# Attention in trips of 64 queries of four batches, with float32 scores in tiles

## The reference

```python
qkv = x @ c_attn_w + c_attn_b                      # q, k, v of the words
k = concat([cond @ uk_w.T + uk_b, k]); v = concat([cond @ uv_w.T + uv_b, v])
scores = q @ k.T / sqrt(32)                        # 16 heads, causal: kj <= qi + 1
x1 = x + (softmax(scores + mask) @ v) @ c_proj_w + c_proj_b
xw = x1 @ Wx + b
h = tanh(h @ Wh + xw[t])                           # 512 steps, all batches at once
out = x1 + h
```

## Time and profile before

| | us |
|---|---|
| three runs, median | 1697.04 (1691.76 to 1697.95) |
| the profiled execution | 1689.44 |
| its span, first to last instruction | 1687.6 |
| PE busy | 1521.2 (90%) |
| PE weight loads | 1288.2 (76%) |
| DVE, ACT, POOL busy | 817.9, 718.4, 369.9 (48%, 43%, 22%) |

### The profile page before, as it was taken

The page is one execution under the profiler, slowest core; times in us unless marked ns, Lnnn a source line. Parts: engine busy times, 40 slices in busy tenths (PEclk is TensorE's granted clock), DMA queues, the critical chain, the costliest instruction groups (busy, mean ns, idle before and its releaser), DMA issues.

```text
span 1687.6 us, 65682 instructions
## 1 busy us (share of the span) xinstructions
PE 1521.2 (90%) x28397; PEld 1288.2 (76%) x28397; DVE 817.9 (48%) x2592; ACT 718.4 (43%) x2289; POOL 369.9 (22%) x535
## 2 busy tenths in 40 slices
PE   6589988999999999999999988999999999777775
PEld 6478777778877878888888877888888788666664
DVE  4455554454545455555555545555565555222221
ACT  3355553444444444544445444454454545111111
POOL 2045552203131222203132130311313100000000
PEclk9799899999999999999999999999999999999999
DMA  7655555334344454445545445555555632000000
GB/s 252 184 186 179 166 181 145 111 96 124 106 126 116 120 145 132 129 110 144 143 137 151 112 136 148 142 156 133 151 140 156 165 89 70 9 15 10 15 9 15
DMA packets 139936, 204.73 MB, mean 121 GB/s; under 512 B 19432, under 2 KB 91240, under 8 KB 139136
## 3 DMA queue, kind: packets, MB, share of 16 engines
q1 hardware_dynamic: 112640, 128.05, 28.9%
q0 software_dynamic: 27008, 72.47, 13.0%
HBM read 133.06 MB, written 67.37 MB: 119 GB/s over the span
## 4 chain that ended last, share of the span: by engine, by line
PE 79%; DMA 6%; DVE 5%; issue 4%; ACT 4%; SPq 2%; POOL 0%; DVEq 0%; ACTq 0%; POOLq 0%
PE rec L1004 24%; PE turned L938 10%; PE dense L466 7%; PE dense L467 6%; PE dense L468 6%; PE rec L995 5%; PE scores L928 5%; PE pv L951 4%; PE scores L1004 4%; DMA xin<-x 3%; DVE pre L842 3%; ACT states L694 2%; PE pv L969 2%; DMA kq<-kq_dram 1%; PE dense L1011 1%
## 5 line engine op out<-in xcount | busy, mean ns | idle before, releaser
L1004 PE MATMUL rec<-wh,states 128*32 128x128 f32 x14336 | 485.2, 276 | 62.9 <-ACT states L694 61.3
L1004 PEld LDWEIGHTS rec<-wh,states 128*32 128x32 f32 x14336 | 376.0, 110 | 129.1 <-ACT states L694 90.7
L648 ACT ACTIVATE probs<-probs,nmax 128x128 f32<-128x128 f32 (+3 forms) x512 | 287.4, 562 | 209.5 <-DVE nmax L791 203.0
L694 ACT ACTIVATE states<-pre 128x32 f32<-128x32 f32 x512 | 133.3, 260 | 431.3 <-DVE pre L842 430.3
L842 DVE STREAM_TRANSPOSE pre<-rec 128x128 f32<-128x128 f32 x448 | 141.6, 316 | 342.1 <-PE rec L1004 338.9
L791 DVE CUSTOM_DVE_ANT_0 probs<-scores,msk,nimg 128x128 f32<-128x128 f32 (+3 forms) x512 | 276.2, 544 | 61.8 <-PE scores L928 54.5
L938 PE MATMUL turned<-ident,probs 128*128 128x128 f32 x1280 | 243.7, 290 | 13.1 <-ACT probsT L655 11.7
L928 PE MATMUL scores<-kq 96*128 96x128 f32 (+3 forms) x512 | 204.9, 403 | 18.5 <-DMA kq<-kq_dram 16.7
L938 PEld LDWEIGHTS turned<-ident,probs 128*128 128x128 f32 x1280 | 145.4, 141 | 78.8 <-issue 55.7
L800 DVE COPY probsT<-turned 128x128 f32<-128x128 f32 (+3 forms) x256 | 124.6, 487 | 80.1 <-PE turned L938 75.7
L655 ACT COPY probsT<-turned 128x128 f32<-128x128 f32 (+3 forms) x256 | 107.0, 418 | 95.8 <-PE turned L938 94.2
(11 more groups left out here) (159 smaller groups left out, 2218.6 us busy)
## 6 DMA issues: line engine op xcount, KB each, us to landing
kq<-kq_dram SPq DMA_DIRECT2D x96, 320.0 KB, 5.2
kq<-kq_dram SPq DMA_DIRECT2D x96, 256.0 KB, 4.4
kq<-kq_dram SPq DMA_DIRECT2D x96, 192.0 KB, 3.6
kq_dram<-qs_hi POOLq DMA_DIRECT2D x120, 128.0 KB, 2.9
kq_dram<-ks_hi POOLq DMA_DIRECT2D x120, 128.0 KB, 3.4
kq<-kq_dram SPq DMA_DIRECT2D x96, 128.0 KB, 2.8
xin<-x SPq DMA_DIRECT2D x32, 256.0 KB, 4.0
v_dram<-vbuf POOLq DMA_DIRECT2D x32, 256.0 KB, 3.1
```

The lines of the kernel that those rows point to most:

```text
L648: act.activation(probs[:, g % PROBS, 0:n], probs[:, g % PROBS, 0:n], ACT.Exp, scale=-1.0, bias=nmax[:, e, h:h + 1], accum_out=rowsum[:, e, ...
L694: act.activation(state_cells(g), pre[:].rearrange("p f (b z) -> p f b z", z=GROUP)[:, :, :, s], ACT.Tanh).then_inc(h_ready, 1)
L1004: last = pe.matmul(rec_bank(g // GROUP)[Q * j:Q * j + Q, 0:P], state_tile(g - 1)[:, f, :], wh[:, f, P * j:P * j + P], start=False, stop=f ...
```

## The change

A trip is now 64 queries of four batches, `PARTS` = 8 parts by `QUADS` = 2, still 16 trips of 32 units. Part p sees 64 (p+1) keys, so the last stretch without attention has 64 steps, and 448 steps are spread over 14 trips. A unit is one head of two batches, 64 queries each, in the two halves of the 128 partitions.

- q stays in SBUF in float32; k is stored once in float32, by one DMA a chunk on SP's queue, and loaded by one DMA a group of four heads for two batches.
- A score is two float32 matmuls of 32 rows by 64 columns, one for each batch; head j of a group lies in rows 32 j. Units u and u+1 are put behind each other in PE's order.
- The values product has for each tile of keys and each head one matmul for each of two batches, of 64 columns each. Values are loaded in two or four DMAs into two buffers.
- A number of keys that is not a multiple of 128 leaves a last tile of 64 keys in transposes and values product.
- The image score is float32 on two tiles of 64 columns. x is loaded by four DMAs with runs of 64 queries. ACT makes q, DVE makes k. The split of x moves from unit 14 or 15 to 15 or 16, the chunks from 15 or 17 to 16 or 18.
- In the setup the raw weights lie elsewhere, and SP no longer waits ahead of the projection's weights.

```diff
-TRIPS = BLOCKS * PAIRS
+W = P // 2
+PARTS = S // W
+QUADS = 2
+PAIRED = 2
+TRIPS = PARTS * QUADS
 UNITS = 2 * H
 HEADS = TRIPS * UNITS
 GROUPS = HEADS // HC
-STEPS = S // (BLOCKS * PAIRS)
+STEPS = W // QUADS
...
-FIRST = (BLOCKS - 1) * P
-PROBS = 4
+FIRST = S - W
+PROBS = 5
 TURNED = 6
-ROOM = 2 * HC * (P + S)
+ROOM = 3 * 2 * S
 LOADS = 5
-FREE = (7, 5, 5, 5, 5)
-SPLIT_AT = (15, 14, 14, 14, 14)
-VTILES = 3
+SPLIT_AT = (16, 16, 15, 15, 15, 15, 15, 15)
+CHUNK_AT = (18, 18, 16, 16, 16, 16, 16, 16)
+VTILES = 2
...
-        size = HC * P * (block_of(group // 8) + 2)
+        size = 2 * keys(group // 8)
...
+            emit([("pv", v, 0, 0.1 + 0.213 * keys(v // 8) / P)])
         if TURN_LAG <= u < HEADS + TURN_LAG:
             v = u - TURN_LAG
-            emit([("turn", v, 0, 0.05 + 0.11 * (block_of(v // UNITS) + 1))])
+            emit([("turn", v, 0, 0.05 + 0.11 * tiles_of(v // UNITS))])
         if u < HEADS:
+            if u % 2 == 0:
+                emit([("score", v, 0, 0.07 + 0.107 * keys(g) / P) for v in (u, u + 1)])
             if u % HC == HC - 1:
                 loads += [("kqload", group, 0, 0.0) for group in range(GROUPS) if PLACES[group][0] == u // HC + 1]
-            emit([("score", u, 0, max(0.11, 0.053 * (block_of(g) + 1)) + 0.1)])
...
-        qs_hi = sb("qs_hi", [P, 2, 2 * P], F32R)
-        qs_lo = sb("qs_lo", [P, 2, 2 * P], F32R)
-        ks_hi = sb("ks_hi", [P, 2, 2 * P], F32R)
-        ks_lo = sb("ks_lo", [P, 2, 2 * P], F32R)
-        kq_tiles = sb("kq", [P, ROOM], F32R)
-        vbuf = sb("vbuf", [P, 2 * D + VTILES * BLOCKS * P])
+        q = sb("q", [P, 2, C, 2 * P])
+        knew = sb("knew", [P, C, 2 * P])
+        k_tiles = sb("kt", [P, ROOM])
...
-        kq_dram = nc.dram_tensor("kq_dram", [3, PAIRS, P, C, 2, P + S], F32, kind="Internal").ap()
+        k_dram = nc.dram_tensor("k_dram", [B, C, P, S], F32, kind="Internal").ap()
...
-        def store_parts(eng, kind, g, i):
-            p, r = divmod(g, PAIRS)
-            if kind == "q":
-                parts, at, stored = (qs_hi, qs_hi, qs_lo), 0, q_stored if g else q_stored_first
-            else:
-                parts, at, stored = (ks_hi, ks_lo, ks_hi), P * (p + 1), k_stored if g else k_stored_first
-            for part, src in enumerate(parts):
-                eng.dma_start(kq_dram[part, r, :, i, :, at:at + P],
-                              src[:, i % 2, :].bitcast(F32).rearrange("p (e t) -> p e t", e=2)
-                              ).then_inc(stored[i % 2], 16)
-        def wait_stored(eng, kind, parity, n):
-            first, later = (q_stored_first, q_stored) if kind == "q" else (k_stored_first, k_stored)
-            if n > 2:
-                eng.wait_ge(later[parity], 48 * (n - 2))
-            else:
-                eng.wait_ge(first[parity], 48 * n)
+        def store_keys(eng, g, i, stored):
+            p, r = divmod(g, QUADS)
+            eng.dma_start(k_dram[4 * r:4 * r + 4, i, :, W * p:W * p + W].rearrange("b p t -> p b t"),
+                          knew[:, i, :].rearrange("p (b t) -> p b t", b=4)).then_inc(stored, 16)
...
+        def load_x(eng, g):
+            p, r = divmod(g, QUADS)
+            for k in range(2):
+                for pair in range(PAIRED):
+                    eng.dma_start(xin[:, g % 2, pair, 2 * k:2 * k + 2, :].rearrange("p f (e t) -> p (f e) t", e=2),
+                                  x[p // 2 * PAIRS + 2 * r + pair, :, 2 * k:2 * k + 2, :]
+                                  .rearrange("p f (e t) -> p (f e) t", e=2)[:, :, W * (p % 2):W * (p % 2) + W]
+                                  ).then_inc(x_loaded[g % 2][k], 16)
...
-                    for part in range(3):
-                        sp.dma_start(heads_tile(g)[Q * part:Q * part + Q].bitcast(F32),
-                                     kq_dram[part, r, :, c, e, 0:P + P * (p + 1)]
-                                     .rearrange("(j d) t -> d j t", d=Q)).then_inc(tile_loaded[g % LOADS], 16)
+                    sp.dma_start(heads_tile(g), k_dram[4 * r + 2 * e:4 * r + 2 * e + 2, c, :, 0:keys(trip)]
+                                 .rearrange("b p t -> p b t")).then_inc(tile_loaded[g % LOADS], 16)
...
+                    whole, left = divmod(keys(trip), P)
+                    for b in range(2):
+                        mine = v_dram[4 * r + 2 * e + b, 0:keys(trip), P * c:P * c + P]
+                        if whole:
+                            sp.dma_start(vtile[g % VTILES][:, b, 0:whole, :],
+                                         mine[0:P * whole].rearrange("(n q) d -> q n d", q=P)
+                                         ).then_inc(v_loaded[g % VTILES], 16)
...
+                    act.activation(q[:, g % 2, i, :], bank(kind, g, i)[:, 0:2 * P], ACT.Identity,
+                                   bias=bqk[:, 0, i:i + 1]).then_inc(copied(kind, g, i), 1)
...
+                    dve.tensor_scalar(knew[:, i, :], bank(kind, g, i)[:, 0:2 * P], bqk[:, 1, i:i + 1], None,
+                                      ALU.add).then_inc(copied(kind, g, i), 1)
...
-                        pe.wait_ge(tile_loaded[group % LOADS], 48 * (group // LOADS + 1))
+                        if e == 0:
+                            wait_copied(pe, "q", trip, c)
+                        pe.wait_ge(tile_loaded[group % LOADS], 16 * (group // LOADS + 1))
                     if g > 1:
                         pe.wait_ge(shifted_ready, g - 1)
-                    pe.matmul(scores[g % 2][:, 0:n], heads_tile(group)[0:3 * Q, j, 0:P],
-                              heads_tile(group)[0:3 * Q, j, P:P + n], start=True, stop=True).then_inc(scores_ready, 1)
+                    rows = slice(Q * j, Q * j + Q)
+                    for b in range(2):
+                        at = W * (2 * e + b)
+                        last = pe.matmul(scores[g % 2][W * b:W * b + W, 0:n], q[rows, trip % 2, c, at:at + W],
+                                         heads_tile(group)[rows, b, :], start=True, stop=True, skip_group_check=True)
+                    last.then_inc(scores_ready, 1)
...
-                    for k in range(p + 1):
-                        last = pe.transpose(turned[g % 2][:, P * k:P * k + P], probs[:, g % PROBS, P * k:P * k + P], ident[:])
+                    for at in range(0, n, P):
+                        last = pe.transpose(turned[g % 2][0:min(P, n - at), at:at + P],
+                                            probs[:, g % PROBS, at:min(at + P, n)], ident[:])
...
-                    for k in range(p + 1):
-                        for j in range(HC):
-                            last = pe.matmul(pv[Q * j:Q * j + Q, P * c:P * c + P],
-                                             vtile[g % VTILES][:, k, Q * j:Q * j + Q],
-                                             probsT[:, (HC * g + j) % TURNED, P * k:P * k + P],
-                                             start=c == 0 and k == 0, stop=False, skip_group_check=True)
+                    for at in range(0, n, P):
+                        rows = slice(0, min(P, n - at))
+                        for b in range(2):
+                            mine = slice(at + W * b, at + W * b + W)
+                            for j in range(HC):
+                                last = pe.matmul(pv[Q * j:Q * j + Q, P * c + W * b:P * c + W * b + W],
+                                                 vtile[g % VTILES][rows, b, at // P, Q * j:Q * j + Q],
+                                                 probsT[rows, (HC * g + j) % TURNED, mine],
+                                                 start=c == 0 and b == 0 and at == 0, stop=False, skip_group_check=True)
```

More of the change, by code:

```diff
@@ L49 @@
 WEIGHT_LOADS = 16 * 2
[L50 removed]
+SETUP_LOADS = 16 * 9
 SPLITS = (0, 2, 4, 6, 1, 3, 5, 7)
 LAGS = {
[L56 removed]
+    "DVE": {"xsplit": 0.7, "k": 0.2, "v": 0.2, "imgscore": 0.2, "score": 0.2, "turn": 0.2, "imgprob": 0.0,
             "total": 0.5, "norm": 0.2, "attnlow": 0.9, "proj": 0.2, "step": 0.1, "hist": 0.8,
             "vimg": 0.2, "wproj": 0.8},
[L59 removed]
+    "ACT": {"xsplit": 0.0, "q": 0.2, "score": 0.8, "turn": 0.2, "imgprob": 0.2, "imgturn": 0.2,
             "rowturn": 0.2, "norm": 0.6, "step": 0.5, "out": 0.2, "wproj": 0.0},
[L61 to L62 removed]
+    "POOL": {"mskload": 0.9, "mskscale": 1.0, "vstore": 1.0, "out": 1.0, "vimg": 1.6},
+    "SP": {"xload": 0.8, "vimgload": 0.9, "k": 0.7, "kqload": 0.8, "vload": 0.5},
 }
@@ L68, in block_of, with keys, tiles_of @@
 def block_of(g):
-    return g // PAIRS
+    return g // QUADS
+def keys(g):
+    return W * (block_of(g) + 1)
+def tiles_of(g):
+    return -(-keys(g) // P)
 def tile_places():
@@ L86, with v_loads @@
 PLACES = tile_places()
+def v_loads():
+    counts = []
+    for group in range(GROUPS):
+        n = keys(group // 8)
+        mine = 2 * (n // P > 0) + 2 * (n % P > 0)
+        counts.append(mine + (counts[group - VTILES] if group >= VTILES else 0))
+    return counts
+V_LOADS = v_loads()
 def main_order():
@@ L176, in order @@
     place = {}
-    for b in range(BLOCKS - 1):
```

(41 more changed lines are left out.)

231 lines of the change are left out of this document (103 added, 128 removed).

## The result

The changed kernel takes 1740.35 us (median of four runs, 1732.76 to 1741.58), the kernel before 1695.55 (1691.76 to 1697.95): a ratio of 1.0257, 95% interval 1.0221 to 1.0293. It is 2.6% slower; the forecast was 1747 in an own range of 1706 to 1788. The profiled execution took 1741.58 us, 52 more than the one before; forecast was +50.

A forecast was written before the change was run, and what follows sets the result against it. PE was taken as the bound. Scores +127, steps -34 and waits -43 summed to +50 us on the profiled 1689.4 us, 1739, or 1747 against the median; own range 1706 to 1788, 8 in 10 range 1685 to 1850.

The forecast's parts named there:

- Bound: Whole kernel: PE's work decides the time until only the recurrence is left; PE holds 79% of the last chain.
- Scores, +127: Scores on PE: 77 us of old scores go, 204 us of paired float32 scores come, +127 us.
- cut pairs: Steps falling between two heads of a score pair: 43 pairs lose their overlap of row groups, +24 us.
- the price around a pair: Around each score pair: changes of array shape and first weights in the open, 0.24 us, 61 us for 256 pairs.
- Steps, -34: Recurrence: 64 steps leave the tail, -116 us, and join the PE-bound part, +82 us; net -34 us.
- Values product, 0: Values product on PE: twice the matmuls at half the columns, groups of four at 0.055 us, no change.
- The rival of +70: Values product: groups of four keep their 0.11 us, +70 us, giving 1817 us; chance 0.10.
- Image scores, 0 within 5: Image scores on PE: float32 on two tiles costs the same as before, 0 within 5 us either way.
- Waits, -43: PE's idle time: waits at the start, for keys, x and first-stage products given back, clock included, -43 us.
- Off PE, 0 to 20: Other engines and queues: nothing moves while PE is the bound; 0 us, up to 20 for late loads.
- The price of a changed shape: PE's array: changing its shape costs 0.21 us in and out, from steps on 128x32 tiles.
- The rival "free": Score tiles: they change the array's shape for nothing, -61 us, giving 1686 us; chance 0.15.

The follow-up runs named there:

- run 1: Changed kernel with one score at a time in PE's order instead of two heads behind each other: 1875.06 us, ratio 1.1095.
- run 2: Changed kernel with each step that would fall between the two heads of a pair put behind the second: 1703.29 us, ratio 1.0064.
- Run 3: Changed kernel with the last 128 steps run alone in the tail again, as in the kernel before: 1774.13 us, ratio 1.0485.
- run 6: Changed kernel with the 64 stores of keys issued by GpSimd's queue instead of SyncE's: 1732.54 us, ratio 1.0233.
- run 12: Changed kernel with no pair cut by a step and the stores of keys on GpSimd's queue: 1693.34 us, ratio 1.001.
- run 8: Changed kernel without cut pairs, each step moved nearby to where it adds the fewest changes of the array's shape: 1713.31 us, ratio 1.012.
- run 7: Changed kernel with the split of x and the chunks one unit earlier: 1799.01 us, ratio 1.063.
- run 5: Kernel before, with the split of x and the chunks behind it one unit later: 1661.43 us, ratio 0.9828.

## Why the prediction was right, point by point

- **Bound.** Right: PE was the bound and the change gave it work. DVE, ACT and SyncE end no large wait of PE in the middle.
- **Scores, +127.** Scores and transposes together measured +123.9. Full overlap of the tiles was right (run 1). Two terms were off and cancelled. With 0.108 us for a transpose alone, 138 us of both sums are transposes: the old scores cost 136 and not 77 (0.19, 0.24, 0.29 and 0.36 us in the mean at the four sizes), since I had read 0.06 to 0.24 us where score and transpose overlapped best, and the new ones cost 260 and not 204. In the latter, cut pairs are 57 and not 43 and cost 41 us and not 24 (run 2): a cut pair pays first weights and changes of shape again besides its stream. These are 17 of the 56 us. Another 13 are the price around a pair: by the rows above 0.91 + 0.58 for pair and four transposes, less 0.43 and 0.77, is 0.29 and not 0.24 (no run shows its 0.03 for first weights apart). The other 26 aren't priced apart. In them are the lower clock from 50 to 180 us (0.80, it was 0.88) and the price of entering the tiles ahead of steps and values products, which a distance between starts puts on the transpose in front.
- **Steps, -34.** Measured -113.2 in the tail (forecast -116) and +73.3 ahead of it (+82): -40. Run 3 gives +51 for the way back by tail and steps, +34 with all that follows from it.
- **Values product, 0.** +8.5 us. Groups of four did go to half: 16 of them take 1253.24 - 1252.08 = 1.16 us with the change behind, 0.07 each. The half-filled tile is a shape of its own (64 rows by 32 columns) and pays once more: from a record of 128 rows to one of 64 it is 0.149 us, between records of one shape 0.014, in 48 places, 6.5 of the 8.5 us. The rival of +70 falls.
- **Image scores, 0 within 5.** -7.1. **Half-filled transposes, 0**: not visible apart.
- **Projections.** Not in the sum: +13.9 us, mostly in the first of each three products (line 488); their number and columns are the same. What changed is what stands ahead of a group of products. Score and first two products, before and after:

```profile
1041.86 0.48 PE L928 MATMUL scores<-kq 96*128 96x512 f32 x1
1042.17 0.28 PE L466 MATMUL dense<-attnT_hi,wproj_hi 128*128 128x256 f32 x1
1042.29 0.28 PE L467 MATMUL dense<-attnT_lo,wproj_hi 128*128 128x256 f32 x1
```

```profile
1243.65 0.97 PE L953 MATMUL scores<-kt,q 32*64 32x448 f32 x4
1244.55 0.39 PE L488 MATMUL dense<-xT_hi,wqkv_hi 128*128 128x256 f32 x1
1244.77 0.29 PE L489 MATMUL dense<-xT_lo,wqkv_hi 128*128 128x256 f32 x1
```

Behind the old score the first product takes 0.12 us, as every product of 256 columns does; behind a score tile it takes 0.22, and behind a transpose 0.20 (there the last transpose takes 0.03 instead of 0.11 in turn). 189 of 242 groups began behind a score in the kernel before; 95 of 238 now begin behind a score tile and 93 behind a transpose: 95 x 0.10 + 93 x 0.08 = 17 us. So this belongs to the change of the scores, and with it they cost some 138 us and not the 127 of the forecast.
- **Waits, -43.** The idle time fell by 49.1 where the sum had 35 without the clock; the 8 us for a better clock didn't come (0.89 after, 0.90 before in the first stage). The first score came at 40.9 us, not 43.
- **Off PE, 0 to 20.** SyncE's stores, hidden in the forecast, cost 4 to 9 us by runs 6 and 12.
- **The price of a changed shape.** The rival "free" falls: 0.08 us each in run 8, where rows 5 had 0.21 for two. The Trainium skill (TensorEngine Tiling (Array Packing), Tiling Modes) says that a change of mode drains the engine; run 8 agrees that it costs, and its longer idle time shows that it isn't the dearest thing here.

So the sum was right to 2 us by errors of 59 and 56 us that cancel within the scores, and of +24 us (projections, values, the rest) against -22 (steps, image scores, waits and 3 of the scores) outside. The mechanism was right (PE bound, tiles that overlap fully, a dear pair against a shorter tail); that the size was, is in good part luck.

## What to carry to other kernels

Pack units that share the array only if nothing can come between them: one condition in the order was worth 33 to 37 of the 45 us (by the ratios and by the medians). Before a layout is changed to save stores and splits on engines with room, find the one wait in which such an engine stands with its queue behind it: moving the split of x by one unit made the kernel before 32 us faster, while the change at its best order only came level with it (run 12). A second unit later gave nothing, and one unit earlier cost the changed kernel 59. Price an instruction by a sum over all its places, not by the distance at one place that overlaps well.

## What the runs showed of the hardware

- Four tiles of 32 rows by 64 columns in float32, two row groups by two column groups, run at the price of one row group: 0.91 and 0.90 us at 448 keys.
- A change of the array's shape costs about 0.1 us: 0.08 in the mean over 153 of them at a clock of 1.00 (runs 2 and 8), half of 0.21 in the earlier trace rows, 0.10 for the first product behind a score tile.
- Short waits of PE cost clock as well. Between 300 and 1400 us the changed kernel, with no wait over 0.7 us, has 1.00 throughout (2.4 GHz); with nine waits of 2.2 to 5.0 us (run 7) it has 0.98 and 0.97, some of the time at 1.2 GHz, 21.5 us in all; and the kernel before loses 3.5 us instead of 13 when most of such waits go (run 5). One of run 7's waits, and its windows ahead of it and around its end:

```profile
892.48 1.29 PE L1025 MATMUL rec<-wx,x 128*32 128x128 f32 x20 [4.97 <-ACT rec L649]
```

```profile
880.00:890.00 10.00, 7.50 (x151) 6.04 (x143) 3.71 (x15) 1.99 (x6) 0.64 (x1) 1.00 0.34 75
890.00:897.00 7.00, 4.52 (x71) 3.53 (x75) 1.91 (x5) 2.22 (x6) 0.00 (x0) 0.51 0.20 55
```

Not each such wait does it: one of 3.0 us in the kernel before (at 653 us) and one of 2.6 in run 7 (at 363) left the clock at 1.00.
- The clock in the first 200 us differs between executions. PE's windows from 90 to 110 us in the changed kernel, and in run 6:

```profile
90.00:100.00 10.00, 9.43 (x90) 6.47 (x86) 3.87 (x25) 4.79 (x24) 0.68 (x2) 0.64 0.25 57
100.00:110.00 10.00, 10.00 (x65) 7.87 (x65) 4.37 (x19) 2.64 (x12) 1.15 (x2) 0.51 0.19 46
```

```profile
90.00:100.00 10.00, 9.53 (x108) 7.19 (x105) 5.75 (x29) 5.60 (x28) 1.83 (x4) 1.00 0.28 68
100.00:110.00 10.00, 6.49 (x79) 5.34 (x78) 5.62 (x32) 1.71 (x7) 1.04 (x2) 0.92 0.37 89
```

The first ran at 1.2 GHz for most of these 20 us (0.64 and 0.51), although PE had been busy since 60 us with a single break of 0.47 us. No row tells why; the four executions of the changed kernel lie 9 us apart, so an effect of that size needs many runs.
